# Softmax shares turned as eight columns and spread over partitions by DMA, and stack fills merged two into one, in a graph attention kernel

## The reference

```python
q, k, v = (proj(Wq, bq), proj(Wk, bk), proj(Wv, bv))        # x @ W.T + b, 8 heads of 32
scores = jnp.einsum('bhqd,bhkd->bhqk', q, k) * SCALE
scores = scores * (adj_matrix + bond_matrix)[:, None, :, :] # both are adj here
attn = jax.nn.softmax(scores, axis=-1)
ctx = jnp.einsum('bhqk,bhkd->bhqd', attn, v)
x = _layernorm(x + (ctx.reshape(b, seq_len, 256) @ Wo.T + bo), axis=-1)
```

## Time and profile before

| | |
|---|---|
| median of 3 runs | 481.57 us (480.04 to 482.72) |
| the profiled execution's own time | 479.8 us |
| its span | 478.0 us |
| busy: PE, DVE, ACT, POOL | 449.9, 399.2, 387.6, 349.6 us |
| DMA | 102.60 MB in 41273 packets |

### The profile page before, as it was taken

One profiled execution on the slowest core, in us unless ns is written; L12 is line 12 of the kernel. 1 busy time (PEld: TensorE's weight loads), 2 busy tenths in 40 slices (PEclk: granted clock), 3 DMA queues, 4 the chain that ended last, 5 costly groups with the idle time before them and its releaser, 6 DMA issues.

```text
span 478.0 us, 13269 instructions
## 1 busy us (share of the span) xinstructions
PE 449.9 (94%) x3846; PEld 382.9 (80%) x3846; DVE 399.2 (84%) x1705; ACT 387.6 (81%) x1257; POOL 349.6 (73%) x480
## 2 busy tenths in 40 slices
PE   4779999999999999999999999999999999999972
PEld 3567988888889888888898888888988888888651
DVE  4157898888898988888989888889898898899961
ACT  5559888888898888889988888889888888888830
POOL 1547576869868696888869686986869688865555
PEclk9998999999999999999999999999999999999986
DMA  7576565857656585857567585756658485563201
GB/s 220 217 268 246 190 232 215 278 208 230 241 194 253 216 281 192 286 188 237 226 216 255 200 298 202 246 218 214 242 216 282 178 302 197 181 236 133 78 27 44
DMA packets 41273, 102.60 MB, mean 215 GB/s; under 512 B 9969, under 2 KB 18162, under 8 KB 41202
## 3 DMA queue, kind: packets, MB, share of 16 engines
q1 hardware_dynamic: 27506, 75.54, 42.0%
q10 hardware_dynamic: 13696, 26.22, 17.8%
HBM read 26.22 MB, written 8.39 MB: 72 GB/s over the span
## 4 chain that ended last, share of the span: by engine, by line
PE 81%; DVE 6%; issue 3%; ACT 3%; SPq 3%; DMA 2%; POOL 1%; POOLq 0%; DVEq 0%
PE turn_bank L241 21%; PE proj_bank L260 17%; PE ctx_bank L303 11%; PE row_bank L229 11%; PE out_bank L317 9%; PE out_bank L276 8%; DVE probs L381 4%; SPq L169 3%; PE inv_bank L288 2%; DMA xt<-in_x_t 2%; ACT probs L486 2%; PE row_bank L260 1%; DVE low_top L389 1%; DVE stats L421 1%; ACT xt_parts L509 0%
## 5 line engine op out<-in xcount | busy, mean ns | idle before, releaser
L486 ACT ACTIVATE probs<-probs,low_top 128x256 f32<-128x256 f32 x512 | 255.7, 503 | 54.8 <-DVE low_top L389 50.6
L381 DVE CUSTOM_DVE_ANT_0 probs<-row_bank,adj_rows 128x256 f32<-128x256 f32 x512 | 191.9, 412 | 15.6 <-PE row_bank L229 13.4
L396 DVE COPY turned_probs<-turn_bank 128x512 f32<-128x512 f32 x192 | 132.1, 688 | 35.7 <-PE turn_bank L241 34.6
L241 PE MATMUL turn_bank<-ident,probs 128*128 128x128 f32 x1024 | 156.2, 275 | 3.5 <-ACT turned_probs L496 1.4
L241 PEld LDWEIGHTS turn_bank<-ident,probs 128*128 128x128 f32 x1024 | 121.3, 141 | 33.8 <-ACT probs L486 17.6
L229 PE MATMUL row_bank<-stack 128*128 128x256 f32 x512 | 123.4, 323 | 3.8 <-issue 2.9
L260 PE MATMUL proj_bank<-xt_parts,w_parts 128*128 128x512 f32 x360 | 105.6, 403 | 3.6 <-POOL xt_parts L606 1.9
L486 ACT ACTIVATION_READ_ACCUMULATOR probs<-probs,low_top 128x1 f32 x512 | 97.5, 190 | 0.0
L600 POOL TENSOR_TENSOR parts<-whole,parts 128x512 fp32r<-128x512 f32 x64 | 82.4, 1288 | 15.9 <-ACT parts L543 10.9
L229 PEld LDWEIGHTS row_bank<-stack 128*128 128x128 f32 x512 | 77.4, 191 | 5.9 <-issue 4.8
L621 POOL CAST ctx_parts<-context 128x512 fp32r<-128x512 f32 x32 | 19.6, 612 | 75.1 <-DVE context L409 75.1
(11 more groups left out here) (45 smaller groups left out, 458.0 us busy)
## 6 DMA issues: line engine op xcount, KB each, us to landing
stack<-parts SPq DMA_DIRECT2D x504, 128.0 KB, 2.5
xt<-in_x_t SPq DMA_DIRECT2D x16, 512.0 KB, 3.5
adj_rows<-in_adj ACTq DMA_DIRECT2D x16, 512.0 KB, 4.2
xr<-in_x ACTq DMA_DIRECT2D x16, 512.0 KB, 5.8
out<-result ACTq DMA_DIRECT2D x32, 256.0 KB, 4.3
stack<-parts ACTq DMA_DIRECT2D x8, 128.0 KB, 2.3
turned_probs<-in_wk SPq DMA_DIRECT2D x1, 256.0 KB, 3.7
turned_probs<-in_wq SPq DMA_DIRECT2D x1, 256.0 KB, 3.0
```

The source lines that it names most:

```text
L241: last = nc.tensor.transpose(turn_bank[o % 2][:, c * S + t * P:c * S + (t + 1) * P], probs[:, o % RING, t * S + c * P:t * S + (c + 1) * P] ...
L381: last = nc.vector.tensor_tensor_reduce(probs[:, o % RING, t * S:(t + 1) * S], row_bank[o % 2][:, t * S:(t + 1) * S], adj_rows[:, (n // 2) ...
L396: nc.vector.tensor_copy(turned_probs[:, (H * g + o) % TURNED, :], turn_bank[o % 2][:]).then_inc(moved_dve, 1)
L486: last = nc.scalar.activation(tile, tile, ACT.Exp, bias=low_top[:, n % 2, o, t:t + 1], accum_out=sums[:, n % 2, t, o:o + 1])
```

## The change

Three things are changed together.

- **The shares' way.** PE transposes `shares` itself, eight columns for each of the two tiles of nodes, in the same step at o = 7 behind `project_out`. ACT copies the 8x256 result to `share_rows` at o = 0 of the next step (`copy_shares`). SP then issues two DMAs (`spread_shares`), each of which reads four partitions of `share_rows` and writes each of them to 32 partitions of `inverse`. DVE's `scale_context` stays at o = 4, and waits for both. POOL's widening and ACT's copy of 128x512 are gone, with the tile `wide`.
- **The fills.** `fill` issues one DMA of 256 KB for two groups, 0 and 2 or 1 and 3: for keys the same part is read twice, for queries two parts. A pair has 16 fill DMAs in place of 32, with the same bytes.
- **SP's order.** Its step g begins with `spread_shares(g - 1)`. The keys of pair (g + 3) // 2 are filled in odd steps as before, the queries of a pair in the even step after.

```diff
         def fill(eng, pair, which, j):
-            for group in range(J):
-                part = group % 2 if which == 0 else group // 2
-                eng.dma_start(stack[group::J, pair % 2, which, j, :].bitcast(F32),
-                              parts[j::J, 2 * which + part, :].bitcast(F32)
-                              ).then_inc(stacked[pair % 2][which][j], 16)
+            for n in range(2):
+                if which == 0:
+                    source = parts[j::J, n:n + 1, :].to_broadcast([D, 2, T * 512])
+                else:
+                    source = parts[j::J, 2:4, :]
+                eng.dma_start(stack[n::2, pair % 2, which, j, :].bitcast(F32),
+                              source.bitcast(F32)).then_inc(stacked[pair % 2][which][j], 16)
...
-            def fill_stacks(pair):
-                for which in range(2):
-                    sp.wait_ge(kq_low, 4 * pair + 2 * which + 2)
...
+            def fill_stack(pair, which):
+                sp.wait_ge(kq_low, 4 * pair + 2 * which + 2)
+                for j in range(J):
+                    if pair > 1:
+                        sp.wait_ge(rows_made, 8 * (2 * pair - 3) + 2 * j + 2)
+                    if pair > 0 or which == 0 or j >= J // 2:
+                        fill(sp, pair, which, j)
+            def spread_shares(g):
+                sp.wait_ge(rows_out, g + 1)
+                wait(sp, ctx_ready, g)
+                for half_ in range(2):
+                    sp.dma_start(inverse[:, half_ * S:(half_ + 1) * S],
+                                 share_rows[J * half_:J * (half_ + 1), :].unsqueeze(1).to_broadcast([J, D, S])
+                                 ).then_inc(inverted, 16)
             def step(g):
-                if g % 2 == 0:
-                    return
-                if is_pair(g + 5):
+                if is_graph(g - 1):
+                    spread_shares(g - 1)
+                if g % 2 == 1 and is_pair(g + 5):
                     load_x_t((g + 5) // 2)
-                if is_pair(g + 3):
-                    fill_stacks((g + 3) // 2)
+                if g % 2 == 1 and is_pair(g + 3):
+                    fill_stack((g + 3) // 2, 0)
+                if g % 2 == 0 and g > 0 and is_pair(g + 2):
+                    fill_stack((g + 2) // 2, 1)
...
             def turn_shares(g):
-                pe.wait_ge(widened, g + 1)
-                wait(pe, inverted, g)
-                for half_ in range(2):
-                    for t in range(T):
-                        last = nc.tensor.transpose(inv_bank[:, half_ * S + t * P:half_ * S + (t + 1) * P],
-                                                   wide[:, t, J * half_:J * (half_ + 1), :].rearrange("p h d -> p (h d)"),
-                                                   ident[:])
-                last.then_inc(inv_made, 1)
+                pe.wait_ge(shares_ready, g + 1)
+                wait(pe, rows_out, g)
+                for t in range(T):
+                    last = nc.tensor.transpose(inv_bank[0:H, t * P:(t + 1) * P], shares[:, t, :], ident[:])
+                last.then_inc(shares_turned, 1)
...
-                    if o == 2 and is_graph(g - 1):
-                        turn_shares(g - 1)
...
                     if o == 7 and is_graph(g - 1):
                         project_out(g - 1)
+                    if o == 7 and is_graph(g):
+                        turn_shares(g)
...
             def scale_context(g):
                 dve.wait_ge(ctx_made, g + 1)
-                dve.wait_ge(inverted, g + 1)
+                dve.wait_ge(inverted, 32 * g + 32)
...
-            def copy_inverse(g):
-                act.wait_ge(inv_made, g + 1)
-                wait(act, ctx_ready, g)
-                nc.scalar.copy(inverse[:], inv_bank[:]).then_inc(inverted, 1)
+            def copy_shares(g):
+                act.wait_ge(shares_turned, g + 1)
+                wait(act, inverted, 32 * g)
+                nc.scalar.copy(share_rows[:], inv_bank[0:H, 0:T * P]).then_inc(rows_out, 1)
...
+                    if o == 0 and is_graph(g - 1):
+                        copy_shares(g - 1)
...
-            def spread_shares(g):
-                pool.wait_ge(shares_ready, g + 1)
-                wait(pool, inv_made, g)
-                nc.gpsimd.tensor_copy(wide[:].rearrange("p t h d -> p (t h) d"),
-                                      shares[:].rearrange("p t h -> p (t h)").unsqueeze(2).to_broadcast([P, T * H, D])
-                                      ).then_inc(widened, 1)
```

More of the change, by code:

```diff
@@ L71, in build @@
         turned_probs = sb("turned_probs", [P, TURNED, T * S])
-        wide = sb("wide", [P, T, H, D])
+        share_rows = sb("share_rows", [H, T * P])
         inverse = sb("inverse", [P, 2 * S])
@@ L107, in build @@
         moved_dve, moved_act = sem("moved_dve"), sem("moved_act")
-        shares_ready, widened, inv_made = sem("shares_ready"), sem("widened"), sem("inv_made")
+        shares_ready, shares_turned, rows_out = sem("shares_ready"), sem("shares_turned"), sem("rows_out")
         ctx_made, inverted, ctx_ready = sem("ctx_made"), sem("inverted"), sem("ctx_ready")
@@ L190, in load_x_t @@
                 sp.dma_start(xt[:].rearrange("p t s -> p (t s)"), x_t[pair]).then_inc(xt_in, 16)
-            def fill_stacks(pair):
-                for which in range(2):
-                    sp.wait_ge(kq_low, 4 * pair + 2 * which + 2)
[L195 to L200, removed]
+            def fill_stack(pair, which):
[12 more added lines that the diff above has]
+                                 ).then_inc(inverted, 16)
             def step(g):
-                if g % 2 == 0:
-                    return
-                if is_pair(g + 5):
+                if is_graph(g - 1):
+                    spread_shares(g - 1)
+                if g % 2 == 1 and is_pair(g + 5):
                     load_x_t((g + 5) // 2)
-                if is_pair(g + 3):
-                    fill_stacks((g + 3) // 2)
+                if g % 2 == 1 and is_pair(g + 3):
+                    fill_stack((g + 3) // 2, 0)
+                if g % 2 == 0 and g > 0 and is_pair(g + 2):
+                    fill_stack((g + 2) // 2, 1)
             load_x_t(1)
-            fill_stacks(0)
+            fill_stack(0, 0)
+            fill_stack(0, 1)
             load_x_t(2)
-            fill_stacks(1)
+            fill_stack(1, 0)
+            fill_stack(1, 1)
             run_steps(step)
@@ L221, in rows @@
                         pe.wait_ge(stacked[(n // 2) % 2][which][o // T],
-                                   (n // 4) * (J * 16) + J * 16)
+                                   (n // 4) * 32 + 32)
                 wait(pe, rows_used, 8 * n + o - 1)
@@ L399, in divide @@
                 dve.wait_ge(probs_ready, H * g + H)
-                wait(dve, widened, g)
+                wait(dve, shares_turned, g)
                 nc.vector.reciprocal(shares[:], sums[:, g % 2]).then_inc(shares_ready, 1)
@@ L573, in step @@
                             read_kq((g + ahead) // 2, KQ_CUT_SLOTS[g % 2, o])
-                    if o == 3 and is_graph(g - 1):
-                        copy_inverse(g - 1)
                     if o == 5 and is_graph(g + 2):
@@ L595, in cut_kq @@
                         for j in range(J):
-                            pool.wait_ge(stacked[(pair - 1) % 2][c // 2][j], ((pair - 1) // 2 + 1) * (J * 16))
+                            pool.wait_ge(stacked[(pair - 1) % 2][c // 2][j], ((pair - 1) // 2 + 1) * 32)
                 if pair > 0:
@@ L671, in step @@
                 for o in range(H):
-                    if o == 7 and is_graph(g):
-                        spread_shares(g)
                     if (g % 2, o) in X_SLOTS and is_pair(g + 4):
```

## The result

The changed kernel takes 785.34 us (median of 4, 784.03 to 786.66) against 481.19 us for the kernel before: ratio 1.632, 95% interval 1.626 to 1.638. The forecast was 585 us with a range of 505 to 620. It had the side and the place right, and was far too small.

The account below looks back on a forecast made before the run. PE bounds the kernel before; after, a loop through SP's fill takes 34.9 us a pair against 27.3, costing 106 us over 14 pairs. 479.8 + 106 - 4 + 2 - 1 = 583, forecast as 585 us, range 505 to 620.

Parts of the forecast that it names:

- What bounds the kernel before: Middle of the kernel: PE sets the time, busy 13.62 and 13.69 us a step; DVE only 1.3 us per graph short.
- PE's part: Shares' turn on PE: four transposes become two, saving 0.22 us a graph, 7.0 us over 32 graphs, if PE stays bound.
- SP's order and the loop: Shares queue behind SP's fill, which waits for scale_context and POOL; the loop sets the pitch, 17.4 us a graph.
- the signs that the prediction named for being wrong: Shares issued before their step's fill, landing under 3 us, or DVE's context showing no wait.
- The other traffic and the fill's data: DMA queues, per pair: 5.5 us of adj, xr, output and similar traffic; 10.4 us for the rest of the fill.
- the shares' term: Two shares DMAs, 0.26 MB a graph: bounds 0.7 us (16 engines) and 2.8 us; 2.8 taken, 5.6 a pair.
- Start and end: Earlier `xt` gains 4 us at the start; the last scale_context comes 2.3 us later at the end.
- A: Rival, chance 0.25: same loop, shares on 16 engines, 30.7 us a pair, 525 us.
- B: Rival, chance 0.15: shares reach `inverse` in time in both steps, PE stays the bound, 470 us.

Follow-up runs that it names:

- the run with sixteen rows in the middle of the fill: Changed kernel, shares written four times, a half's source rows on sixteen partitions 8 apart; SP issues the shares after four of eight fill DMAs: 483.42 us.
- rows 8 apart: Changed kernel, with each half's source rows on partitions 0, 8, 16, 24 or 1, 9, 17, 25 in place of neighbours: 594.78 us in one run.
- the one on ACT's queue: Changed kernel, with a half's source rows on sixteen partitions 8 apart and the shares' DMAs issued by ACT behind `move_turned` at o = 0: 484.88 us.
- rows 32 apart: Changed kernel, with each half's source rows on partitions 0, 32, 64, 96 or 1, 33, 65, 97 in place of neighbours: 651.85 us.

## Why the prediction was wrong

- **What bounds the kernel before**: right, with a flaw. PE was the end of every wait there, and at o = 1 to 5 DVE and ACT were so near behind it that PE had a gap if it worked less. The projection at that point shows it: in the chain of before it takes 0.84 to 0.91 us where the others take 0.69.
- **PE's part** (0.22 us a graph saved): wrong in sign, though it did not matter here. Alone it would cost 0.22 us a graph, 7 us: two transposes less at the old place gained nothing (475.9 against 476.1 us), two more at the new one cost 7.0 us. That the other two of the four gain nothing either is taken from the run with sixteen rows in the middle of the fill (483.4 us).
- **SP's order and the loop** (scale_context, POOL's four operations, the fill, the shares): right. 4.67 us of 4.70 forecast, eight fill DMAs in 5.1 us, scale_context waiting in 31 graphs, PE down from 81% to 15% of the chain, two unequal steps. But the waits are 8.3 us in place of 2 to 5, and the shares land 13.9 and 12.7 us after SP began to issue them, not 5 to 9. None of the signs that the prediction named for being wrong came: the step that failed was not on its list.
- **The other traffic and the fill's data**: right. With rows 8 apart, where the shares' data run as the forecast took them, the pair is 34.9 us in the stretch shown and 35.4 in the mean, and the whole 594.8 against 585.
- **The failed step is the upper bound of the shares' term.** "The bounds are 0.7 us (16 engines) and, if the work is divided as the source's four partitions are, four times that, 2.8 us." It took for granted that an engine keeps its rate, and asked only how many there are. Their number was right: 0.21 of 16 busy fits four, as the section of the Trainium skill cited in the prediction has it. But the rate went with the place of the source rows, and the term measures 0.26 MB at 30 GB/s = 8.7 us. 2 x (8.7 - 2.8) = 11.8 us is what the pair is over the forecast (47.0 - 34.9 = 12.1). That this fits so well is in part luck: from the first packet to the end of the last the shares of this pair took 9.1 and 10.1 us, so the other terms came out 1.5 us shorter together. Over 28 steps the 11.8 us a pair are 165 of the 200 us that were missing. The rest is where the forecast saw little or no loss: the last scale_context starts at 769.61, 12.4 us after its weigh_v at 757.17, where the forecast had 5.5; the first one at 56.6, against 51.8 before, although the first reciprocal came 3.1 us earlier; and the steps without a fill.
- **Start and end**: the start's gain was there (3.1 us at the first reciprocal, 4 forecast), and the kernel with merged fills alone is 5 us faster than before.
- **The rivals**: A was built and gives 551 us with 31.9 us a pair (525 and 30.7 forecast). B was built in two ways, and does not get under the kernel before: in the one with the shares in the middle of the fill its 7 us over merged fills alone are what two more transposes at o = 7 cost by themselves, and the one on ACT's queue is 1.5 us slower still.

What stays open: why the shares' data of one DMA for each head are through 1.4 us sooner, and how much of the gain from four rows to sixteen is engines and how much is ports; neither was tried further.

## What to carry to other kernels

Count a DMA's time three ways and take the longest: bytes by engine rate, by the number of engines it is dealt to, and by the ports behind its source rows (the destination rows were not varied here). When a wait moves to a DMA queue, write down what the queue holds in front of it and what releases that: if it leads back to the waiting instruction, its turn is the new pitch. And taking work from the busiest engine gains only where no chain over the others is as long; one run with that work left out tells this before anything is rebuilt.

## What the runs showed of the hardware

- Two transfers, from partitions 0 to 3 and 4 to 7 one behind the other, moved 30 GB/s with 0.21 of the DMA engines busy and, as eight, 32 GB/s with 0.75. With 0.22 to 0.28 of the engines they moved 52 GB/s from rows 32 apart and 96 GB/s from rows 8 apart; the steady rates of the three were 23, 47 and 98 GB/s.
- A slow transfer holds up the issue of the next: a fill DMA then stood 3.07 us at SP, against 0.60, and in the run with sixteen rows on ACT's queue ACT's compute was late by up to 1.1 us behind its issues, 39 us in all.
- A fill of 64 partitions is issued as quickly as one of 32 (eight in 5.08 us, against 24 in 15.23 us).
- Two transposes less for PE gained nothing at one place (475.9 against 476.1 us), and two more cost 7.0 us at another (483.1 us).
